# Sorted expert rows in two equal groups, queries of two batches beside the expert pairs, key stacks issued behind the gather

## The reference

```
logits = x @ router_w; top 2 of 8; probs = sigmoid(top values)
xin = probs * x                      # per chosen expert
gate, up = split(xin @ gate_up_w[e]); h = silu(gate) * up
out = shared(x) + sum over e of h @ down_w[e]
```

## Time and profile before

| | us |
|---|---|
| median of 3 runs | 808.86 (806.12 to 809.22) |
| the profiled execution | 805.29 |
| its span | 803.2 |
| PE busy | 725.5 (90%) |
| DVE busy | 555.4 (69%) |
| ACT busy | 380.6 (47%) |
| POOL busy | 208.5 (26%) |

### The profile page before, as it was taken

How to read it: one execution, slowest core, us unless ns; L and a number is a source line. 1 busy time by engine, 2 the same in 40 slices (tenths; PEclk the granted TensorE clock), 3 DMA queues, 4 the chain that set the end, 5 groups by cost and what they waited for, 6 DMA issues and landing times.

```text
span 803.2 us, 13098 instructions
## 1 busy us (share of the span) xinstructions
PE 725.5 (90%) x4986; PEld 423.1 (53%) x4987; DVE 555.4 (69%) x1209; ACT 380.6 (47%) x521; POOL 208.5 (26%) x206
## 2 busy tenths in 40 slices
PE   8999899979897787878979999989999999899996
PEld 4446676846686564334434455544455554445434
DVE  4887987625372435777878787777787777887814
ACT  2102334346432230345756665556665566664670
POOL 2497232312651211123400505001505002300000
PEclk9999999999899796789999999999999999999999
DMA  9900001004589435922764491814491810560000
GB/s 293 341 0 1 1 1 48 35 1 180 166 251 234 123 75 100 141 72 40 128 78 69 151 108 62 119 20 60 161 108 54 122 23 2 114 72 15 1 1 14
DMA packets 42185, 71.96 MB, mean 90 GB/s; under 512 B 6309, under 2 KB 29989, under 8 KB 41222
## 3 DMA queue, kind: packets, MB, share of 16 engines
q1 hardware_dynamic: 39384, 60.34, 35.3%
q0 software_dynamic: 2592, 9.12, 4.5%
q10 hardware_dynamic: 144, 1.64, 0.6%
HBM read 48.66 MB, written 22.42 MB: 88 GB/s over the span
## 4 chain that ended last, share of the span: by engine, by line
PE 58%; DVE 16%; issue 13%; DMA 7%; ACT 3%; POOL 2%; SPq 1%; POOLq 0%; DVEq 0%
PE ps L1278 10%; PE ps L1362 9%; PE ps L1342 7%; PE ps L1082 5%; PE ps L1092 4%; DVE small L2061 4%; PE ps L961 3%; DMA y<-yscr,pos 3%; DMA yscr<-r 2%; PE ps L1008 2%; PE ps L1193 2%; PE ps L1051 2%; PE ps L968 2%; PE ps L1039 2%; DVE small L1875 1%
## 5 line engine op out<-in xcount | busy, mean ns | idle before, releaser
L2061 DVE TENSOR_REDUCE small<-ps 128x1 f32<-128x400 f32 (+1 forms) x512 | 284.6, 572 | 92.2 <-PE ps L1278 86.1
L1736 ACT ACTIVATE r<-ps 128x1024 f32<-128x1024 f32 (+1 forms) x208 | 212.5, 1023 | 103.6 <-PE ps L1342 100.7
L1278 PE MATMUL ps<-r 96*128 96x400 bf16 (+1 forms) x512 | 173.8, 347 | 26.7 <-DVE small L2061 16.7
L1362 PE MATMUL ps<-r 128*17 128x256 f32 (+1 forms) x1664 | 132.4, 391 | 1.6 <-ACT r L1736 1.3
L1342 PE MATMUL ps<-r 99*128 99x256 bf16 (+1 forms) x832 | 128.8, 278 | 0.7 <-ACT r L1714 0.7
L1278 PEld LDWEIGHTS ps<-r 96*128 96x128 bf16 x512 | 50.3, 98 | 142.0 <-DVE small L2061 99.9
L1342 PEld LDWEIGHTS ps<-r 99*128 99x128 bf16 (+1 forms) x832 | 82.5, 101 | 33.3 <-issue 10.2
L849 POOL TENSOR_TENSOR r<-r 128x401 bf16<-128x401 f32 (+3 forms) x72 | 66.0, 950 | 105.1 <-ACT r L1586 104.1
L1092 PE MATMUL ps<-wkvT,r 128*128 128x256 f32 (+1 forms) x208 | 59.6, 403 | 2.6 <-ACT r L1597 2.2
L1362 PEld LDWEIGHTS ps<-r 128*17 128x17 f32 (+1 forms) x1664 | 27.8, 96 | 52.2 <-issue 42.4
L1082 PE MATMUL ps<-r,wkvT 128*128 128x400 f32 (+1 forms) x128 | 52.5, 506 | 2.4 <-issue 2.0
(11 more groups left out here) (247 smaller groups left out, 954.1 us busy)
## 6 DMA issues: line engine op xcount, KB each, us to landing
r<-kscr SPq DMA_DIRECT2D x84, 200.1 KB, 8.7
kscr<-r SPq DMA_DIRECT2D x18, 400.2 KB, 3.6
r<-in_ctx_dram SPq DMA_DIRECT2D x3, 1601.0 KB
r<-xscr SPq DMA_DIRECT2D x14, 256.0 KB, 3.8
yscr<-r SPq DMA_DIRECT2D x14, 256.0 KB, 5.0
r<-qscr SPq DMA_DIRECT2D x24, 128.0 KB, 5.2
xscr<-hT SPq DMA_DIRECT2D x1, 2432.0 KB, 21.7
kscr<-r POOLq DMA_DIRECT2D x6, 400.2 KB, 8.7
```

What stands on the lines that cost most here:

```text
L1278: mm(bank(ca % 2)[:, 0:m], qst[0:SROWS, h, q0:q0 + P], kst[0:SROWS, s % 2, h % HALF, a:a + m], start=True, stop=True).then_inc(mx_mm, 1)
L1362: last = mm(bank(6)[32 * k:32 * k + VW, 0:LQ], vx[0:n, b % 2, kt, h, :], pr[i % 3][0:n, k * LQ:(k + 1) * LQ], start=kt == 0, stop=kt == KT ...
L1736: fn(pr[i % 3][0:n, :], bank(2 + 2 * (i % 2), 2)[0:n, :], ACT.Exp, scale=SCALE1)\
L2061: v.tensor_reduce(mxc[quad % 2][:, n:n + 1], bank(ca % 2)[:, 0:m], AX_X, ALU.max).then_inc(mx_rdy, 1)
```

## The change

The groups become tiles 0 to 3 and 4 to 7 (15 sorted tiles each, again 30 in all), and the list of steps puts eight pairs ahead of the other shared-expert steps in place of six. The join and query work of batch 0 go to steps 14 to 18, those of batch 1 come out of quad 0 and go to steps 18 to 23. The first maxima start at step 21 and run over seven steps. On POOL both writes of keys stand together, and each of the two stacks stands behind a gather; the stack of quad 0 also waits for the second write. `fetch` of batches 0 and 1 waits for the first group's last stores. ACT issues the load of batch 1's context at step 13. On PE and ACT the turn of the second pair of tiles moves ahead of route(0). DVE takes the statistics in halves of four tiles.

```diff
-GROUPS = ((0, 2), (2, TILES))
+GROUPS = ((0, TILES // 2), (TILES // 2, TILES))
...
-ITEMS = [("s", 0)] + [("x", i) for i in range(6)] + [("s", 1), ("s", 2), ("s", 3)] + [("x", i) for i in range(6, PAIRS)]
+ITEMS = [("s", 0)] + [("x", i) for i in range(8)] + [("s", 1), ("s", 2), ("s", 3)] + [("x", i) for i in range(8, PAIRS)]
...
-JOINS = (None, 0, 4, 9)
-QSTEPS = (None, 1, 25, 4 * KT + 25)
-QFIRST = (12, 12, 13, 13, 13, 14, 15, 16)
+JOINS = (None, None, 0, 4)
+QSTEPS = (None, None, 25, 4 * KT + 25)
+QFIRST = ((14, 14, 15, 15, 15, 16, 17, 18), (19, 19, 20, 20, 20, 21, 22, 23))
+JFIRST = (14, 18)
...
-FIRST_MAX = NI
-FSTEPS = FIRST_V + (KT + 1) // 2
+FIRST_MAX = NI + 2
+FSTEPS = FIRST_MAX + 7
+CONTEXT = NI - 6
...
@@ beside_experts
-    beside.setdefault(12, []).append(("query", 0, "join"))
-    for at, (_, part) in zip(QFIRST, QPARTS):
-        beside.setdefault(at, []).append(("query", 0, part))
+    for b in range(2):
+        beside.setdefault(JFIRST[b], []).append(("query", b, "join"))
+    for b in range(2):
+        for at, (_, part) in zip(QFIRST[b], QPARTS):
+            beside.setdefault(at, []).append(("query", b, part))
@@ stack_quad
-            eng.wait_ge(*key_parts_out(s))
+            eng.wait_ge(*key_parts_out(max(s, 1)))
@@ sync
-                if n == QFIRST[-1] + 1:
+                if n == QFIRST[0][-1] + 1:
                     write_queries(0)
                     stack_queries(0)
@@ fetch
-                g = 0 if b == 0 else 1
-                last = SORTED[0] // 2 if b == 0 else PAIRS - 1
+                g = 0 if 2 * b < GROUPS[0][1] else 1
+                last = SORTED[0] // 2 if g == 0 else PAIRS - 1
@@ gpsimd
             write_keys(pool, 0)
+            write_keys(pool, 1)
+            fetch(0)
             stack_quad(pool, 0)
-            write_keys(pool, 1)
+            rsqrt_query(0)
+            fetch(1)
+            split_queries(0)
             stack_quad(pool, 1)
-            fetch(0)
-            rsqrt_query(0)
-            split_queries(0)
-            fetch(1)
+            rsqrt_query(1)
+            split_queries(1)
             fetch(2)
-            rsqrt_query(1)
             fetch(3)
-            split_queries(1)
             split_keys(2)
@@ tensor (scalar alike)
             first_keys(1, 1)
+            turn_pair(1)
             first_keys(1, 2)
             route(0)
             first_keys(1, 3)
-            for i in range(1, TILES // 2):
+            for i in range(2, TILES // 2):
                 turn_pair(i)
@@ scalar
-            act.dma_start(ctxT, ctx_in[1]).then_inc(ld_ctx, 16)
...
+                if n == CONTEXT:
+                    act.dma_start(ctxT, ctx_in[1]).then_inc(ld_ctx, 16)
@@ vector
-            stats_of(range(2))
+            stats_of(range(TILES // 2))
             moments_of(0)
-            stats_of(range(2, TILES))
+            stats_of(range(TILES // 2, TILES))
```

More of the change, by code:

```diff
@@ L117, in schedule @@
             put(start + 4 * KT + at, "tail", b, part)
-    for b in range(1, B):
+    for b in range(2, B):
         put(JOINS[b], "query", b, "join")
-    for b in range(1, B):
+    for b in range(2, B):
         for at, part in QPARTS:
@@ L1618, in _ @@
             turned_pair(0)
-            for c in range(1, len(CH)):
-                keys_bias(1, c, next(banks67))
-            for i in range(1, TILES // 2):
+            keys_bias(1, 1, next(banks67))
+            turned_pair(1)
+            keys_bias(1, 2, next(banks67))
+            keys_bias(1, 3, next(banks67))
+            for i in range(2, TILES // 2):
                 turned_pair(i)
```

## The result

The changed kernel takes 819.51 us in the median (814.91 to 820.89, 5 runs), the kernel before 808.86 (806.12 to 813.75, 5 runs). The ratio is 1.014, with a 95% interval of 1.010 to 1.019: 1.4% slower, and outside the range of 793 to 810. Of the forecast's rivals it comes nearest to D (813), which named the right place, "the turn of pair 13 or 14". D's own condition for that time was not met: the step there was 8.4 us longer than a step of 3.3, not 10.8, and the load landed 15.49 us after its issue, not 20. The profiled execution has a span of 813.1 us against 803.2: 9.9 us more.

A forecast was written before the change was run, and what follows sets the result against it. PE, nearly full after the first quad, bounds the kernel; the room lies ahead, in waits for joins and transfers. −0.7 at shift(0) and −6.1 in quad 0 give −6.8 us: span 796.4, forecast 802, range 793 to 810.

The forecast's parts named there:

- D: Steps 13 to 17: context load, stack_quad(0), gather and pair loads meet, stalling PE; 809, or 813 if over 0.5% slower; chance 0.14.
- start: Up to gate_up(0): second power and scaling wait behind eight scatters; +2.8 us, bounds +1 and +4, gate_up(0) at 217.7.
- twelve steps: gate_up(0) to gate_up(12): nine steps with sorted pairs before and after, so again 40.0 us.
- gate_up(12) to turn_q(0): Query 0 beside steps 14 to 18: seven 3.3 us steps, 1 us of PE idle; turn_q(0) at 281.5, −6.1 us.
- transfer of the queries: turn_q(0) to stacked queries: 17.5 us plus 3.5 for sharing DMA engines with stack_quad(1), bounds 0 and +6.5; stacked at 302.5.
- maxima: Stacked queries to shift(0): query 1 takes turns with values on bank 7; +2 us, bounds −2 and +5.
- quad 0: shift(0) to shift(1): join 1 and query 1 gone, 31 us against 37.1, −6.1, bounds −9 and 0.
- The store of pair 7: Batch 0's last store, ahead of its gather: lands in 2 to 3 us, not 14.95, with key stacks behind the gather.
- the join: Batch 0's join at step 14: gather to join 8.04 us, so at 267 when DVE reaches it, no stall.
- Rival C: Quad 0: join(3) at step 4 stalls as join(2) did, quad 0 keeps some 35 us; 806 to 808, chance 0.20.
- the store that took 14.95 us: Reading of the kernel before: a 256 KB store beside key stacks took 14.95 us, against 2.12 with little beside it.
- the quads behind 367.80: Quads after quad 0: nothing in the diff touches them, so they keep their length, 25.80 us for a 13-step quad.

The follow-up runs named there:

- experiment 4: Changed kernel with sigmoid_power(1) after the first four of group 0's eight scatters; 1.011 of the kernel before.
- 7: Kernel before with the groups of four tiles, eight pairs ahead of the other shared steps and fetch(1) from the first group; 1.008 of the kernel before.
- kernel 11: Kernel before with key stacks behind the gather, stack_quad(1) behind a wait for the stacked queries, first maxima at steps 21 to 26; 0.989 of the kernel before.
- 12: Kernel 11 with the groups of four tiles added; 1.000 of the kernel before.
- Experiment 1: Changed kernel with the load of batch 1's context back ahead of step 0; 0.998 of the kernel before, median 808.19 us.
- 2: Changed kernel with stack_quad(1) behind rsqrt_query(1) and a wait for batch 0's stacked queries; 1.003 of the kernel before.
- 8: Kernel before with POOL's order alone changed: both key writes, fetch(0), stack_quad(0), query 0 work, stack_quad(1), fetch(1); 0.994 of the kernel before.
- 9: Kernel before with key stacks behind the gather and stack_quad(1) behind a wait for batch 0's stacked queries; 0.991 of the kernel before, median 796.90 us.
- 13: Changed kernel with project_q and turn_q of query 1 at steps 25 and 26 in place of 22 and 23; 1.011 of the kernel before.
- 14: Changed kernel with context load first, stack_quad(1) late, join(3) at step 9, project_q and turn_q of query 1 at steps 25 and 26; 0.997 of the kernel before.
- 5: Changed kernel with the context load ahead of step 0 and stack_quad(1) behind the wait for batch 0's stacked queries; 1.000 of the kernel before.
- 6: Changed kernel with context load ahead of step 0, stack_quad(1) behind the stacked queries, join(3) at step 9 instead of 4; 0.994 of the kernel before.
- 10: Kernel before with the first maxima alone moved two steps later, to steps 21 to 27; 0.993 of the kernel before.

## Why the prediction was wrong

Two steps of the prediction failed. The sum had no term for the meeting of stack_quad(0) and the context load with the load of pair 13, and it put the meeting of stack_quad(1) with the query write at +3.5 us. The runs showed one step of 11.66 us for the first and +7.4 us for the second. The forecast span was 796.4 us and the measured one 813.1. The 16.7 us between them are: start +1.4, twelve steps +1.1 (41.06 for 40.0), gate_up(12) to turn_q(0) +9.0 (32.78 for 23.8), transfer of the queries +4.1, maxima +1.5, quad 0 -1.1, and the rest +0.8.

**The start** was forecast at +2.8 us and measured at +4.2. The mechanism in front of it (the power behind eight scatters) was there to 1 us, 211.38 for 210.6. The forecast was short by 0.8 us in the start of the scatters and by 0.6 us behind the scaling, where values(0,6) took 1.97 us at the low clock after 5.99 us of idle time; it took 1.08 before. But the power isn't the only cause: with it early the first sorted rows are late instead, and the fifth step starts at the same time (experiment 4). The groups by themselves cost 0.8% (7), and 1.1% on top of kernel 11 (12). That the first sorted rows come later because there are twice as many scatters was not a term of the sum.

**Steps 13 to 17** hold the largest miss. The only idle time in the sum there was 1 us for the query work, and "the moved transfers meet" was a rival at 0.14. The load of pair 13 took 15.49 us, 11.66 us were spent in one step, and turn_q(0) came at 293.0 for 281.5. What spoke against the rival was sized by bytes: 2.8 MB are 11 us of DMA time. But three steps of slack are only 10 us, so the two are equal, and the bytes are not shared in proportion (last section). Experiment 1 removed the wait with the context load alone, and 5.0 of the 9.0 us; the other 4.0 stay there, with the query's own chain and the low clock behind it, so the 1 us for that was too small as well. The store of pair 7 landed in 1.83 us, as forecast. The gather behind it, with stack_quad(0) issued right after it, was issued last at 264.51 and let the join start at 274.74, 10.2 us later, against 3.34 before; the join was forecast at 267.

**The transfer of the queries** was forecast at +3.5 us with a bound of +6.5 and took +7.4, outside the bound. The mechanism was right (2, 8 and 9 take it in and out: 25.1 and 17.1, 25.8 and 16.7), the size wrong: 1.2 MB were spread over a chain of 17.5 us, but they fell on its one small write, 8.42 us for 1.97. The full 4.8 us of the Trainium skill's rule was nearer and still short.

**The first maxima**: +3.5 for +2, within the bounds. The turns of query 1 on bank 7 cost about 3 to 4 us (13, 14). The rest is not explained by the idle time ahead: with that cut from 9.63 to 2.58 and 2.80 us the stretch still takes 30.1 and 29.1 us (5, 6). That the maxima gain 4.6 us when they alone are moved (10) was not seen: the forecast had a bound of -2 for it.

**Quad 0**: -7.2 for -6.1, right. Rival C, the stall that moves to join(3), didn't happen in the changed kernel, and did once the rest was mended (5).

**Readings of the forecast** that don't hold: the store that took 14.95 us is one of two of 128 KB and not of 256 KB, so it is not like for like with the 2.12 us of a 256 KB store; and the diff does touch the quads behind 367.80, by the 1.5 us named under the result.

So the parts are, against the kernel before: groups +0.8%, POOL's order -0.6%, maxima later -0.7%, each alone. The three gains of the change (order, maxima, query 1 out of quad 0) were undone by the groups, the context load at step 13, and stack_quad(1) beside the query write. Without the last two and with join(3) at step 9 the change is 0.6% faster than the kernel before (6). The kernel before with POOL's order, the late stack_quad(1) and the later maxima alone is 1.1% faster (11). What stays open is how much of the 1.6% of experiment 1 is the pair load. Open too are the quads behind shift(1), where single stretches mostly have one of two lengths (from shift(3) to shift(4) about 26.5 or 28.4 us, from shift(4) to shift(5) 29.4 or 30.8, from shift(12) to shift(13) 25.1 or 26.4) in profiles of kernels with and without the change. The longer ones make up most of the 6.7 us of experiment 9, and hide the gain of the first quad here.

## What to carry to other kernels

When transfers are moved out of one window, list what else runs in the window that they go to, and compare landing times with the slack in steps, not bytes with a mean bandwidth. Keep a bulk transfer from starting with a small write on a chain of waits: here a wait on the chain's own semaphore ahead of the bulk one gave back 8 to 9 us of the chain (2, 9). A gain ahead of a stretch may uncover the next wait there (join(3) at step 4): look for it in the profile of the version with the gain.

## What the hardware showed that was not expected

Sharing was very unequal in bytes. Between 272 and 278 us of the changed kernel the load of pair 13 is under way beside stack_quad(0). The rows are the DMA queues of POOL (q0) and SP (q1): packets, MB, share of the 16 engines' time:

```profile
q0 software_dynamic: 196, 0.83, 75.4%
q1 hardware_dynamic: 196, 0.19, 22.4%
```

Both queues passed the same number of packets, and SP's are a quarter of the size (1.0 KB against 4.2), so SP got a fifth of the bytes. In the kernel before, between 250 and 255 us, where the slow store is under way beside the key stacks, the counts are 223 and 223. The Trainium skill (DMA: Bandwidth & Descriptors, Queues, rings and completion order) says that an engine takes turns between the queues packet by packet, and these counts agree.

The write of the queries (384 KB, 0.48 KB a packet) is another case. Beside stack_quad(1), whose packets have 4.5 KB on the mean, it had these rows between 299 and 304 us, and between 304 and 307.81, when it landed:

```profile
q0 software_dynamic: 124, 0.55, 51.0%
q1 hardware_dynamic: 771, 0.37, 50.1%
...
q0 software_dynamic: 119, 0.55, 106.7%
q1 hardware_dynamic: 45, 0.02, 3.4%
```

By these rows the turns are not one for one: six packets of the write pass for one of the stack, and each queue has half of the engines' time. Then the last 0.02 MB of the write take 3.8 us beside the stack. So the write took four to five times its 1.97 us (8.42 to 10.30 us in four profiles). Why its last packets are so late is not shown, and no other packet size was tried.

Executions of one kernel spread over up to 1.5% here (before: 798.12 to 810.04 us in one set), so a single profile tells a mechanism and its place, not the size of a change in the time.
